# A fused attention and quantised-FFN stage on one core: an integer bf16 product that VectorE scales in PSUM, and a new order of work on three engines

## The reference

```
x += tanh(g_xattn[0]) * attention0(layernorm(x), ctx)        # 16 heads of 8
x += tanh(g_ffn[0])   * mixture_of_experts(layernorm(x))     # 8 experts, top 2
x += tanh(g_xattn[1]) * attention1(layernorm(x), ctx, mask)  # 16 heads of 64
x += tanh(g_ffn[1])   * bit_ffn(layernorm(x))
```

```
h = bit_linear(x, w1)               # 128 -> 512
h = silu(conv over 3 rows (h) + b)  # per feature, within one sequence
y = bit_linear(h, w2)               # 512 -> 128
bit_linear(x, w): xq = clip(round(x * 127 / max|x|), -128, 127) * max|x| / 127   # per row
                  wq = clip(round(w / mean|w|), -1, 1) * mean|w|
```

## Time and profile before

| | us |
|---|---|
| median of three runs (1652.2 to 1660.82) | 1658.28 |
| the profiled execution | 1653.78 |
| its span | 1652.1 |
| PE busy in the span | 1519.5 (92%) |
| DVE busy | 1185.6 (72%) |
| ACT busy | 988.9 (60%) |
| POOL busy | 706.1 (43%) |

### The profile page before, as it was taken

The page is one execution under the profiler, slowest core; times in us unless marked ns, Lnnn a source line. Parts: engine busy times, 40 slices in busy tenths (PEclk is TensorE's granted clock), DMA queues, the critical chain, the costliest instruction groups (busy, mean ns, idle before and its releaser), DMA issues.

```text
span 1652.1 us, 51710 instructions
## 1 busy us (share of the span) xinstructions
PE 1519.5 (92%) x20221; PEld 1236.6 (75%) x20221; DVE 1185.6 (72%) x3076; ACT 988.9 (60%) x1976; POOL 706.1 (43%) x605
## 2 busy tenths in 40 slices
PE   5999999999299999966999999999999999999988
PEld 2777777777289999965787777777777777777764
DVE  5788888897442222217789989898898898887776
ACT  3778878874134444423556666666666666666656
POOL 2335666676511111126765454444544444333320
PEclk9999999996599999987999999999999999999999
DMA  9999960000277777711110000000000000000000
GB/s 282 390 388 380 373 215 26 26 32 32 73 254 226 228 228 229 228 58 34 30 30 18 18 21 20 23 21 21 21 21 21 22 21 18 12 12 12 13 8 23
DMA packets 95625, 169.90 MB, mean 103 GB/s; under 512 B 11984, under 2 KB 43728, under 8 KB 95152
## 3 DMA queue, kind: packets, MB, share of 16 engines
q1 hardware_dynamic: 82800, 140.35, 25.9%
q0 software_dynamic: 11600, 26.10, 4.9%
q10 hardware_dynamic: 1008, 0.40, 0.1%
HBM read 75.71 MB, written 91.10 MB: 101 GB/s over the span
## 4 chain that ended last, share of the span: by engine, by line
PE 23%; DVE 12%; issue 10%; ACT 8%; POOL 2%; DMA 0%; POOLq 0%; ACTq 0%; DVEq 0%
PE L1psM L1209 4%; PE L1psF L1226 3%; PE L1psY L1160 3%; PE L1psY L1167 3%; PE L1psY L1152 2%; ACT L1z L1382 2%; PE L1psS L1178 2%; DVE L1sc L1558 2%; ACT L1OT L1352 2%; DVE L1hs L1607 2%; PE L1psT L1201 2%; DVE L1xd L1507 1%; ACT L1hc L1364 1%; ACT L1hs L1371 1%; PE L1psF L1245 1%
## 5 line engine op out<-in xcount | busy, mean ns | idle before, releaser
L1700 POOL TENSOR_TENSOR L1sc<-L1sc,L1rden 128x1024 f32<-128x1024 f32 x64 | 138.8, 2168 | 269.8 <-DVE L1rden L1574 269.7
L1326 ACT ACTIVATE L1KT<-L1psY 128x512 f32<-128x512 f32 x128 | 77.5, 605 | 246.9 <-PE L1psY L1152 245.7
L926 ACT ACTIVATE GhT<-GpsH,Gwx 128x256 f32<-128x256 f32 x284 | 118.6, 470 | 157.1 <-PE GpsH L894 155.7
L792 POOL TENSOR_TENSOR L0sc<-L0sc,L0top 128x1024 f32<-128x1024 f32 x64 | 121.6, 1900 | 152.3 <-DVE L0top L550 152.1
L1695 POOL TENSOR_TENSOR L1sc<-L1sc,L1top 128x1024 f32<-128x1024 f32 x64 | 121.8, 1904 | 143.4 <-DVE L1top L1565 143.4
L942 DVE TENSOR_TENSOR Gyg<-GpsY,Gwx 128x256 f32<-128x256 f32 x71 | 30.1, 424 | 195.6 <-PE GpsY L902 195.6
L1160 PEld LDWEIGHTS L1psY<-L1xnT,L1WQ 128*128 128x128 f32 x1024 | 128.8, 192 | 30.0 <-issue 25.8
L1152 PE MATMUL L1psY<-L1cx,L1WK 128*128 128x128 f32 x1024 | 137.3, 278 | 12.3 <-DMA L1cx<-in_ctxT 12.3
L997 POOL DMA_DIRECT2D rows_out<-Gyg x71 | 38.4, 541 | 247.7 <-issue 247.7
L1160 PE MATMUL L1psY<-L1xnT,L1WQ 128*128 128x128 f32 x1024 | 141.7, 282 | 0.0
L798 POOL DMA_INDIRECT rows_in<-L0xr,slot x128 | 125.1, 978 | 37.8 <-issue 30.1
(11 more groups left out here) (256 smaller groups left out, 3659.2 us busy)
## 6 DMA issues: line engine op xcount, KB each, us to landing
Gwx<-in_experts SPq DMA_DIRECT2D x71, 579.0 KB, 4.0
rows_in<-L0zero SPq DMA_DIRECT2D x1, 33792.0 KB, 93.3
rows_out<-L0zero SPq DMA_DIRECT2D x1, 33792.0 KB, 191.5
Gxg<-rows_in SPq DMA_DIRECT2D x71, 128.0 KB, 3.5
rows_out<-Gyg POOLq DMA_DIRECT2D x71, 128.0 KB, 3.8
L1cx<-in_ctxT SPq DMA_DIRECT2D x64, 64.0 KB, 1.9
out<-X SPq DMA_DIRECT2D x64, 64.0 KB, 1.8
L0ctxT<-in_ctxT SPq DMA_DIRECT2D x1, 2560.0 KB, 19.9
```

What stands on the lines that cost most here:

```text
L792: nc.gpsimd.tensor_tensor(sc[:, t % 4, :, :], sc[:, t % 4, :, :], top[:, t % 2, :].unsqueeze(2).broadcast_to([P, H, S]), ALU.subtract).the ...
L926: nc.scalar.activation(hT[:, u, m, :], psH[:, u, m, :], ACT.Gelu, bias=wx[:, w, ob1 + m:ob1 + m + 1]).then_inc(s["h_ready"], 1)
L1700: nc.gpsimd.tensor_tensor(sc[:, t % SR, :, :], sc[:, t % SR, :, :], broad(rden[:, t % 2, :]), ALU.mult).then_inc(s["probs_ready"], 1)
```

## The change

The group of four tiles keeps its integers: step 24 of `ffn_in` only takes ROUND off and writes bf16 (`xi`), for the first 14 groups (`INT_GROUPS`). TensorE transposes these in bf16 into bank M (before the scores, not after them), and multiplies them with a bf16 copy of W1. The step of each row, one number per partition, has to become one number per column: `turn_steps` transposes the step's column repeated 128 times, four times a group, into bank F; `take_steps` copies that to SBUF. VectorE's new `scale(n)` multiplies the hidden product in PSUM in place by it, between TensorE and `centre`, once a turn. ScalarE's order changes: rounding goes ahead of the normed tile, `exps` ahead of `centre`, the second Q ahead of the second O. VectorE's order changes: `sums` and `invert` go ahead of `small` part 3 and of the convolution, which before stood ahead of `small` part 2.

```
@@ ffn_in, step 24
+                    if g < INT_GROUPS:
+                        vec.tensor_scalar(xi[:, g % 2, :, :], x, ROUND, None, ALU.subtract).then_inc(s["xq_ready"], 1)
+                        return
                     vec.scalar_tensor_tensor(xq[:, g % 2, :, :], x, ROUND, wide(inv[:, at], G4), ALU.subtract, ALU.mult)
@@ TensorE
+            def turn_steps(g):
+                pe.wait_ge(s["xq_ready"], g + 1)
+                take_bank("F", s["steps_ready"], g + 1)
+                for i in range(G4):
+                    t = G4 * g + i
+                    last = nc.tensor.transpose(psF[:, i * P:(i + 1) * P], inv[:, t:t + 1].broadcast_to([P, P]), ident[:])
+                last.then_inc(s["steps_ps"], 1)
             def hidden(n):
-                mm(ps, W1[:, m * P:(m + 1) * P], xqT[:, g % 2, :], start=True, stop=True).then_inc(s["h_ps"], 1)
+                mm(ps, W1[:, m * P:(m + 1) * P], xiT[:, g % 2, :], start=True, stop=True).then_inc(s["h_ps"], 1)
@@ its loop
                     project(tb)
+                if k >= FX and (k - FX) % G4 == 0 and k - FX < NT:
+                    turn_xq((k - FX) // G4)
                 if tx is not None:
                     scores(tx)
-                if k >= FX and (k - FX) % G4 == 0 and k - FX < NT:
-                    turn_xq((k - FX) // G4)
+                if k >= FX and (k - FX) % G4 == 0 and (k - FX) // G4 < INT_GROUPS:
+                    turn_steps((k - FX) // G4)
@@ ScalarE
+            def take_steps(g):
+                act.wait_ge(s["steps_ps"], g + 1)
+                wait(act, s["h_scaled"], FM * (g - 1))
+                nc.scalar.activation(step[:, g % 2, :], psF[:, :], ACT.Copy).then_inc(s["steps_ready"], 1)
             def centre(n):
-                act.wait_ge(s["h_ps"], n + 1)
+                act.wait_ge(s["h_scaled"], n + 1)
@@ VectorE
+            def scale(n):
+                g = n // FM
+                dve.wait_ge(s["h_ps"], n + 1)
+                dve.wait_ge(s["steps_ready"], g + 1)
+                h = bank("hidden", n)[1]
+                vec.tensor_tensor(h, h, step[:, g % 2, :], ALU.mult).then_inc(s["h_scaled"], 1)
@@ its loop
                 small(k, 0)
                 if tile(k, LN) is not None:
                     layernorm(k)
+                if n is not None:
+                    scale(n)
                 small(k, 1)
+                small(k, 2)
+                if tv is not None:
+                    sums(tv)
+                    invert(tv)
+                small(k, 3)
                 if n is not None:
                     conv_left(n)
                     conv_right(n)
-                small(k, 2)
-                if tv is not None:
-                    sums(tv)
-                small(k, 3)
-                if tv is not None:
-                    invert(tv)
                 if n2 is not None:
                     twice_silu(n2)
@@ prepare, while the experts run
+                    if i == 0:
+                        link(vec.tensor_scalar(ffn["W1b"][:], W1[:], 1.0, None, ALU.mult))
```

More of the change, by code:

```diff
@@ L1017, in attention_ffn @@
         WQ, WK, WV, WO, bias, bo = att["WQ"], att["WK"], att["WV"], att["WO"], att["bias"], att["bo"]
-        W1, W2q, taps, cb, wmean, W3 = ffn["W1"], ffn["W2"], ffn["taps"], ffn["bias"], ffn["scale"], ffn["W3"]
+        W1, W2q, taps, cb, wmean, W3 = ffn["W1b"], ffn["W2"], ffn["taps"], ffn["bias"], ffn["scale"], ffn["W3"]
         W = G4 * P
@@ L1041, in attention_ffn @@
         xqT = sb("xqT", [P, 2, W])
+        xi = sb("xi", [P, 2, G4, D], BF16)
+        xiT = sb("xiT", [P, 2, W], BF16)
+        step = sb("step", [P, 2, W])
+        identb, identh = sb("identb", [P, P], BF16), sb("identh", [P, P], F16)
         am, inv, scl, mul = (sb(n, [P, NT]) for n in ("am", "inv", "scl", "mul"))
@@ L1093, in bank @@
         def bank(stage, t):
-            if t + {"xq": FX, "hidden": FH, "turn": FT, "back": FB, "project": FB}[stage] < LAST:
+            if stage == "xq":
+                return ("M", psM[:, 2:4, :]) if t // G4 < INT_GROUPS else ("F", psF[:, :])
+            if t + {"hidden": FH, "turn": FT, "back": FB, "project": FB}[stage] < LAST:
                 return ("M", psM[:, 2:4, :]) if stage == "back" else ("F", psF[:, :])
@@ L1102, in bank, with halves @@
                 return f"Y{t % 2}", psY[:, t % 2, :]
-            return {"xq": ("F", psF[:, :]), "project": ("M", psM[:, 2, :])}[stage]
-        def halves(ps):
-            return (flat(ps) if len(ps.shape) == 3 else ps).bitcast(F16)[:, 0:W]
+            return "M", psM[:, 2, :]
+        def halves(ps, dt):
+            v = (flat(ps) if len(ps.shape) == 3 else ps).bitcast(dt)
+            return v[:, 0:W]
         def tile(k, lag):
@@ L1216, in turn_xq @@
                 take_bank(name, s["xqT_ready"], g + 1)
+                if g < INT_GROUPS:
+                    ps = halves(ps, BF16)
+                x, eye = (xi, identb) if g < INT_GROUPS else (xq, ident)
                 for i in range(G4):
-                    last = nc.tensor.transpose(ps[:, i * P:(i + 1) * P], xq[:, g % 2, i, :], ident[:])
+                    last = nc.tensor.transpose(ps[:, i * P:(i + 1) * P], x[:, g % 2, i, :], eye[:])
                 last.then_inc(s["x_ps"], 1)
+            def turn_steps(g):
[5 more added lines that the diff above has]
+                last.then_inc(s["steps_ps"], 1)
             def hidden(n):
@@ L1398, in _ @@
                     take_probs(tt, 0)
+                if tile(k - 1, FT) is not None:
+                    rounding(tile(k - 1, FT))
                 if tx is not None:
                     take_xnT(tx)
-                if tile(k - 1, FT) is not None:
-                    rounding(tile(k - 1, FT))
                 if tt is not None:
@@ L1406, in _ @@
                     take_k(tx, 1)
+                if tv is not None:
+                    exps(tv)
                 if n is not None:
                     centre(n)
-                if tv is not None:
-                    exps(tv)
                 if tx is not None:
@@ L1414, in _ @@
                     take_o(tt, 0)
-                    take_o(tt, 1)
                 if tx is not None:
                     take_q(tx, 1)
+                if tt is not None:
+                    take_o(tt, 1)
                 if n2 is not None:
@@ L1426, in _ @@
                     take_xqT((k - FX) // G4)
+                    if (k - FX) // G4 < INT_GROUPS:
+                        take_steps((k - FX) // G4)
             rounding(LAST - 1 - FT)
@@ L1631, in _ @@
             vec.memset(nround[:, 1:2], -1536.0)
+            vec.tensor_scalar(identb[:], ident[:], 1.0, None, ALU.mult)
             vec.tensor_scalar(identh[:], ident[:], 1.0, None, ALU.mult).then_inc(s["consts"], 1)
```

19 lines of the change are left out of this document (12 added, 7 removed).

## The result

After the change the kernel takes 1630.47 us (median of four runs, 1629.41 to 1635.33) against 1657.94 for the kernel before beside it: a ratio of 0.9854, with a 95% interval of 0.9825 to 0.9884 (the ratio is taken over all executions; the two medians alone give 0.983). I had forecast 1675, that is slower; it became faster by 1.5%. The profiled execution took 1629.41 us (1653.78 before). One profile further down, that of `rounding_before`, is of a slower execution (1719 us, where that kernel's others take about 1698), so only its turns are read.

The account below looks back on a forecast made before the run. TensorE bounds, VectorE close behind. Turns 17 to 55 add 14.6 us, 56 to 66 add 3, 11 to 16 add 2: +19, 1673 for the profiled execution, 1675 for a median; range 1640 to 1688.

Parts of the forecast that it names:

- The step that failed: VectorE after `invert`: the second small step starts 0.03 us after `normalise` and stands still; turn 40 becomes 14.05 us, not 13.09.
- the first rival: The second small step gets through and only `twice_silu` stands still: -14 us, 1642; chance 0.28.
- The mechanism: VectorE operations on SBUF stand still during GpSimd's `normalise`, PSUM-reading ones don't; `project` waits for `conv_right`'s bank, 1261.35 instead of 1260.23.
- The undisturbed turn: A turn in which nothing stands still was to take 12.7 us instead of 13.09.
- ScalarE caps the gain: ScalarE's path to `take_z` holds up `project`, so an undisturbed turn gains 0.38 us, not TensorE's 0.65.
- `turn_xq` and `turn_steps`: TensorE's transposes: `turn_xq` falls from 0.57 to about 0.33 us, `turn_steps` adds 0.43; turns 2 and 6 summed with 0.33 + 0.57.
- `scale`: VectorE's new operation was to cost 0.68 us (0.6 to 0.8), 56 times, and still fit into VectorE's time.
- turns 1 and 5 bound by late sums: Large small steps on VectorE delay `sums` and the bank for `project`: turn 1 takes 13.4 us, turn 5 14.0.
- `exps` hides `scale`: `exps` fills ScalarE during `scale`, so `centre` isn't later than ScalarE gets to it.
- The exchange of Q and O: Taking the second Q one copy (0.48 us) sooner on ScalarE was counted as 0, at best 0.27.
- the fourth rival: TensorE alone counts, the change taken at face value: -33 us, 1623; chance 0.03.
- my objection to it: Against TensorE alone counting: ScalarE's path, and VectorE's 103.1 us in eight turns would leave it no idle time.

Follow-up runs that it names:

- rounding_before: The changed kernel with the normed tile ahead of rounding on ScalarE, as before the change; ratio 0.9886 to the kernel before.
- held_256: The changed kernel with a VectorE reduction over 256 SBUF elements ahead of small steps 7 and 16; ratio 1.0028 to the kernel before.
- small3_last: The changed kernel with part 3 of the small steps behind the convolution instead of ahead of it; 1620.89 us, ratio 0.9768 to the kernel before.
- q_before: The changed kernel with both takes of O ahead of the second take of Q, as before the change; ratio 0.9888 to the kernel before.
- third set: Four variants run on a chip of their own, with the kernel before beside them; ratios 0.9796, 0.9886, 0.9888 and 1.0025.
- z_ahead_of_tanh: The kernel of small3_last with `take_z` before tanh on ScalarE; ratio 0.9796 to the kernel before.

## Why the prediction was wrong

In the forecast's own parts, for the profiled execution (1673 forecast, 1629.4 measured): turns 17 to 55 came out at 508.6 instead of 526.2 + 14.6 = 540.8, that is 32.2 less; turns 56 to 65 (up to the start of 66) at 123.6 instead of 133.9, 10.3 less; turns 11 to 16 at 73.4 instead of 77.5, 4.1 less; the rest 2.7 more.

- **The step that failed** is "the second depends on it and follows 0.19 later, at `invert` + 0.36, which is 0.03 after GpSimd's start": it follows 0.14 later, at + 0.31, 0.02 before. I took the distance between two small steps from the earlier trace rows, where the first runs 0.15 and more; right behind a reciprocal it runs 0.10. `held_256` shows what the 0.05 us were worth: 1.3 us in each of 19 turns from 17 to 64, 25 us, and 27.4 of stage with turns 12 and 16. I named this as the first rival with a chance of 0.28, but let a 0.03 margin, made of two sums of rounded rows, carry a chance of 0.50. Which side of `normalise` the step fell on was a matter of hundredths, and no row of the kernel before could tell it. In turn 7 the same step of the argument was right (third step at + 0.37, 1.88 us).
- **The mechanism was right.** A VectorE operation with two SBUF inputs, or an SBUF to SBUF `tensor_scalar`, that starts behind GpSimd's start stands still to its end, taps don't, and `project` waits for the bank: turn 7, `held_256` and `small3_last` show each piece. The rule that I named from the Trainium skill (GPSIMD Engine Reference, Key points) agrees with these rows; they put the price at 1.7 to 1.9 us even for 128x4 elements.
- **The undisturbed turn** was mis-sized: 12.7 forecast, 12.46 measured, and before 13.09. Of the 0.63, 0.47 lie at `project` (hidden + 6.22 before, + 5.75 after) and 0.16 from K to hidden (3.12 before, 2.96 after). That ScalarE caps the gain was right: the product costs 0.21 from start to start (1151.83 to 1152.04), not 0.28, so TensorE saves 0.72, and `project` waits for `take_z` (0.18 idle ahead of L1284 in all quiet turns). `take_z` came 4.98 behind the product's own row, about as I had it (1259.1 - 1254.04 = 5.06). So 0.47 of the 0.72 count, where I had 0.38 of 0.65; and the earlier rounding comes on top, which I had taken off in turns that stand still and left out in the others. With the stall, turns 0, 3 and 4 are 13.78 (`held_256`), not 14.0.
- **`turn_xq` and `turn_steps`** together cost 0.61 (turns 2 and 6 against 0 and 3), not 0.90. TensorE of turn 34:

```profile
1170.73 0.40 PE L1284 MATMUL L1psF<-F_W,L1qT 128*128 128x128 bf16 x4 [0.19 <-ACT L1qT L1420]
1170.96 0.39 PE L1230 MATMUL L1psM<-L1identb,L1xi 128*128 128x128 bf16 x4
1172.37 0.65 PE L1239 MATMUL L1psF<-ident,L1inv 128*128 128x128 f32 x4
1172.86 1.95 PE L1218 MATMUL L1psM<-L1WO,L1OT 128*128 128x128 f32 x16
```

  `turn_xq` starts 0.23 after `project`, whose four small products I had at 0.33, and `turn_steps` takes 0.49 (1172.37 to 1172.86); the forecast priced it at 0.43 in one place and entered 0.57 in the turns. This, with the shorter quiet turn, is the 0.5 by which turns 2 and 6 were too high.
- **Right**: `scale` 0.72 (forecast 0.68, 0.6 to 0.8); that it still fits into VectorE; turns 1 and 5 bound by late sums, 13.18 and 13.82 (13.4 and 14.0); `exps` hides `scale`: `centre` waits for it 2.5 us in 35 turns altogether. The exchange of Q and O is worth 0 with the bf16 product (`q_before`).
- **The nearest number** was the fourth rival's, 1623, with a chance of 0.03, and that is luck: its reason, that TensorE alone counts, isn't what happened, since three turns of eight still wait for VectorE. But my objection to it was wrong too. I had VectorE occupied for up to 103.1 us in eight turns; it is busy 94.9 of 104.3 now, and was busy 95.9 of 108.0 before.
- **What I didn't see** is the cost of not making the moves: with `scale` in, the old order of VectorE costs 40 us of stage and the old one of ScalarE 49. I compared the new orders with the old kernel, where they bring 5.

How the 44 us divide between the failed step and the sizes: 27 by `held_256`; the other 17 are the sizes, above all the shorter quiet turn and the cheaper transposes. The first is measured, the second is what is left. Neither alone explains the miss: without the failed step the sum gives the first rival's 1642, still 12 us too high, and with the stall real (`held_256`) the kernel is as fast as before within 0.5% and not 1% slower.

## What to carry to other kernels

Where a stall is decided by which of two instructions starts first, work out the start of each in hundredths from rows with the same instruction in front; if the margin is below what such rows scatter, give both cases even chances, and look for an order that doesn't hang on it (here: PSUM-reading operations directly behind the one that releases GpSimd, small SBUF steps behind them, worth another 11 us of stage). An engine's queue ahead of a critical instruction is a fixed sum only if none of its entries waits for the engine that the change makes faster. Orders of work and a new operation are to be priced together: the orders alone brought 5 us of stage, the product and `scale` with one engine's old order lost 14 or 24, and both together brought 26.

## What the runs showed that was not expected

- A 128x4 VectorE operation right behind a 128x16 reciprocal runs 0.10 us instead of 0.16, and the one that depends on it starts 0.14 after it instead of 0.18 to 0.20.
- The edge is sharp: started 0.02 before GpSimd's operation a step takes 0.16 us; 0.04 after it, 1.88. A reduction of 256 columns (0.41 us) started 0.14 before isn't lengthened.
- The fp32 product of 512 columns takes 0.93 us of TensorE's time, the bf16 one 0.21: below the four bf16 products of 128 columns (0.33 in the earlier trace rows, 0.23 ahead of L1230).
- On the chip of the third set TensorE shows gaps that nothing in the profile explains inside the values' products, in all four kernels, and the stages before took some 50 us longer. From start to start these products take 1.09 us in each of turns 32 to 39 of the change; there they take mostly 1.4 to 2.0, and 1.1 to 1.3 in turns 3 and 7. One such row, from `z_ahead_of_tanh`:

```profile
1235.91 0.73 PE L1210 MATMUL L1psT<-L1PT,L1V 64*64 64x64 f32 x29 [0.21 <-issue]
```

  Turns 0, 2, 4 and 6 are 0.2 to 0.6 us longer there (12.76 instead of 12.46 in turn 0). The cause is open.
